# A two-layer transformer kernel: top-4 routing for four token blocks at once, and softmax sums read by the logarithm from PSUM

## The reference

```python
# layer 0: attention with 16 query and 4 key/value heads of 64, rotary embedding, no mask
attn = softmax(Q @ K.T / 8);  s = (attn @ V) @ Wo
# layer 0: feed-forward with 16 experts of width 512, plus a shared one of width 1024
scores = sigmoid(x @ router_weight.T)              # T x 16
# 2 of 4 groups by the sum of their two best scores; the others are set to 0
_, tidx = top_k(masked, 4)
tw = scores[tidx];  tw = 2.5 * tw / (sum(tw) + 1e-20)
routed = sum over experts of combine[t, e] * (silu(x @ gate_e) * (x @ up_e)) @ down_e
# layer 1: attention with 16 heads of 64 and a causal mask, with biases
# layer 1: feed-forward of width 3072 with integer weights * (1/127)
```

## Time and profile before

| what | value |
|---|---|
| timed runs | 5173.84 and 5219.94 us, median 5196.89 |
| profiled execution, slowest core | 4995.61 us |
| its span on the core read here (6), first to last instruction | 4994.0 us |
| spans of all cores | 4978.8 to 4994.0 us |
| TensorE matmul busy | 3663.9 us (73%), 14712 instructions |
| VectorE busy | 1323.1 us (26%), 2280 |
| ScalarE busy | 1394.9 us (28%), 1637 |
| chain that ended last | TensorE 53%, DMA 15%, VectorE 15%, ScalarE 10%, issue 5% |

### The profile page before, as it was taken

How to read it: one execution, slowest core, us unless ns; L and a number is a source line. 1 busy time by engine, 2 the same in 40 slices (tenths; PEclk the granted TensorE clock), 3 DMA queues, 4 the chain that set the end, 5 groups by cost and what they waited for, 6 DMA issues and landing times.

```text
span 4994.0 us, 44866 instructions; the slowest of 8 cores (4978.8 to 4994.0 us)
## 1 busy us (share of the span) xinstructions
PE 3663.9 (73%) x14712; PEld 1453.4 (29%) x14712; DVE 1323.1 (26%) x2280; ACT 1394.9 (28%) x1637; POOL 283.0 (6%) x522
## 2 busy tenths in 40 slices
PE   2126766799999999986777777742999966567775
PEld 0012222344434444432222222211444422122221
DVE  3442321033023113212122222225101023443332
ACT  1000000011011011103666666621111101555663
POOL 1000000000000000000000000001101000000000
PEclk7558888899999999998889888865999999889998
DMA  2127777844434434430011111134444420222122
GB/s 65 51 78 194 203 205 187 198 146 143 149 130 144 152 135 144 144 121 11 13 32 36 32 36 32 34 72 116 69 83 68 76 47 7 34 41 57 34 49 44
DMA packets 139090, 450.95 MB, mean 90 GB/s; under 512 B 15568, under 2 KB 15728, under 8 KB 122480
## 3 DMA queue, kind: packets, MB, share of 16 engines
q0 software_dynamic: 73632, 218.42, 21.3%
q1 hardware_dynamic: 65232, 229.67, 13.5%
HBM read 490.23 MB, written 73.40 MB: 113 GB/s over the span
## 4 chain that ended last, share of the span: by engine, by line
PE 53%; DMA 15%; DVE 15%; ACT 10%; issue 5%; DVEq 1%; SPq 0%; ACTq 0%; POOL 0%; POOLq 0%
ACT a16t L1481 9%; PE pst L738 8%; PE pst L752 8%; PE pst L854 4%; PE pb L854 4%; DMA a32t<-l_u 4%; PE pb L995 3%; PE pb L1430 3%; PE pst L931 3%; PE pst L942 3%; PE pst L1453 3%; PE pst L1458 2%; PE pb L1435 2%; PE pst L1347 2%; DMA a16t<-s_g 2%
## 5 line engine op out<-in xcount | busy, mean ns | idle before, releaser
L1481 ACT ACTIVATE a16t<-pst 128x1024 bf16<-128x1024 f32 x832 | 852.1, 1024 | 545.9 <-PE pst L1458 477.3
L738 PE MATMUL pst<-xn_sb,a16t 128*128 128x512 bf16 x2304 | 598.5, 407 | 177.1 <-DVE a16t L686 153.2
L752 PE MATMUL pst<-xn_sb,a16t 128*128 128x512 bf16 x2304 | 565.7, 390 | 0.0
L1430 PE MATMUL pb<-a16t 128*65 128x512 bf16 x832 | 343.9, 413 | 288.0 <-DVE a16t L1576 118.7
L765 ACT ACTIVATE a32t<-pst 128x512 f32<-128x512 f32 x288 | 172.0, 597 | 1103.6 <-PE pst L738 1103.6
L773 DVE TENSOR_TENSOR a32t<-a32t,pst 128x512 f32<-128x512 f32 x256 | 176.1, 688 | 1138.1 <-PE pst L752 1138.1
L1453 PE MATMUL pst<-a16t 128*128 128x512 bf16 x832 | 354.7, 426 | 162.6 <-DVE a16t L1392 103.8
L738 PEld LDWEIGHTS pst<-xn_sb,a16t 128*128 128x128 bf16 x2304 | 226.7, 102 | 496.2 <-issue 277.6
L1458 PE MATMUL pst<-a16t 128*128 128x512 bf16 x832 | 352.5, 424 | 0.0
L1435 PE MATMUL pb<-a16t 128*65 128x512 bf16 x832 | 344.6, 414 | 0.0
L752 PEld LDWEIGHTS pst<-xn_sb,a16t 128*128 128x128 bf16 x2304 | 232.5, 101 | 296.9 <-issue 44.6
(11 more groups left out here) (157 smaller groups left out, 2896.6 us busy)
## 6 DMA issues: line engine op xcount, KB each, us to landing
a16t<-s_g POOLq DMA_DIRECT2D x108, 512.0 KB, 5.0
a16t<-s_u SPq DMA_DIRECT2D x108, 512.0 KB, 4.2
a32t<-l_u SPq DMA_DIRECT2D x32, 1024.0 KB, 9.9
a16t<-s_d SPq DMA_DIRECT2D x27, 1024.0 KB, 5.6
a16t<-s_d POOLq DMA_DIRECT2D x27, 1024.0 KB, 6.1
s_g<-a16t SPq DMA_DIRECT2D x36, 512.0 KB, 7.4
s_u<-a16t SPq DMA_DIRECT2D x36, 512.0 KB, 8.4
s_d<-a16t SPq DMA_DIRECT2D x18, 1024.0 KB, 7.4
```

The source lines that it names most:

```text
L738: li = t.matmul(pb[gp_][:, :], a16t[:, o_gb[wp] + hc * 256 + ici * 128: o_gb[wp] + hc * 256 + ici * 128 + 128], xn_sb[:, hc * T + tc * TC: ...
L752: li = t.matmul(pb[up_][:, :], a16t[:, o_ub[wp] + hc * 256 + ici * 128: o_ub[wp] + hc * 256 + ici * 128 + 128], xn_sb[:, hc * T + tc * TC: ...
L1430: t.matmul(pb4[0:65, :], a16t[:, o_vtm + kc * 65 * nvh + kva * 65: o_vtm + kc * 65 * nvh + kva * 65 + 65], a16t[:, o_pt[kp]:o_pt[kp] + TC] ...
L1481: return s.activation(a16t[:, o_pt[kp]:o_pt[kp] + 2 * TC], pst[kp][:, 0:1024], AF.Exp, scale=0.125)
```

## The change

In stage A0, `f_top4` runs once per chunk on all 64 columns. The working arrays are viewed as 4 groups of 16. Maximum and sum reduce each group to one column (four results); the compares, which took the maximum as a per-partition scalar, are now two-tensor instructions whose second operand repeats the group's value 16 times; the final scale does the same with the reciprocal. The four transposes and the four copies stay, but stand behind the one top-4 operation instead of between four.

In stage C, of both layers, the two copies of the softmax sums and the one logarithm over 1024 columns go; two logarithms of 512 columns read the sums from PSUM instead. Operation `sums` is gone; those that named it now name `rcp`.

```diff
--- before.py
+++ after.py
@@ -531,42 +531,49 @@
                         return li
                     op_rt2 = P.add("V", f_rt2, deps=[op_rt1], name=f"A0rt2{tc}")
 
+                    def f_top4(v):
+                        cur = a32t[:, o_rs + 0:o_rs + 64]
+                        cur3 = cur.rearrange("p (g e) -> p g e", e=16)
+                        selb = a32t[:, o_rs + 64:o_rs + 128]
+                        selb3 = selb.rearrange("p (g e) -> p g e", e=16)
+                        ci = a32t[:, o_rs + 128:o_rs + 132]
+                        ci3 = ci.rearrange("p (g e) -> p g e", e=1)
+                        cib = ci3.broadcast_to((128, 4, 16))
+                        ci2 = a32t[:, o_rs + 132:o_rs + 136]
+                        ci2b = ci2.rearrange("p (g e) -> p g e", e=1)\
+                            .broadcast_to((128, 4, 16))
+                        mk = a32t[:, o_z:o_z + 64]
+                        mk3 = mk.rearrange("p (g e) -> p g e", e=16)
+                        sc3 = a32t[:, o_sc:o_sc + 64]
+                        Ct3 = a32t[:, o_Ct:o_Ct + 64].rearrange(
+                            "p (g e) -> p g e", e=16)
+                        v.tensor_copy(cur, mk)
+                        for _ in range(3):
+                            v.drain()
+                            v.reduce_max(ci3, cur3, axis=AX.X)
+                            v.drain()
+                            v.tensor_tensor(selb3, cur3, cib, ALU.is_ge)
+                            v.drain()
+                            v.scalar_tensor_tensor(cur, selb, -1e9, cur,
+                                                   ALU.mult, ALU.add)
+                        v.drain()
+                        v.reduce_max(ci3, cur3, axis=AX.X)
+                        v.drain()
+                        v.tensor_tensor(selb3, mk3, cib, ALU.is_ge)
+                        v.drain()
+                        v.tensor_tensor(cur, selb, sc3, ALU.mult)
+                        v.drain()
+                        v.reduce_sum(ci3, cur3, axis=AX.X)
+                        v.drain()
+                        v.tensor_scalar(ci, ci, 1e-20, None, ALU.add)
+                        v.drain()
+                        v.reciprocal(ci2, ci)
+                        v.drain()
+                        return v.scalar_tensor_tensor(Ct3, cur3, 2.5, ci2b,
+                                                      ALU.mult, ALU.mult)
+                    op_t4 = P.add("V", f_top4, deps=[op_rt2], name=f"A0t4{tc}")
+
                     for tt in range(4):
-                        def f_top4(v, tt=tt):
-                            cur = a32t[:, o_rs + rCUR:o_rs + rCUR + 16]
-                            ci = a32t[:, o_rs + rCI:o_rs + rCI + 1]
-                            ci2 = a32t[:, o_rs + rCI + 1:o_rs + rCI + 2]
-                            selb = a32t[:, o_rs + rSB:o_rs + rSB + 16]
-                            mk = a32t[:, o_z + tt * 16: o_z + (tt + 1) * 16]
-                            v.tensor_copy(cur, mk)
-                            for _ in range(3):
-                                v.drain()
-                                v.reduce_max(ci, cur, axis=AX.X)
-                                v.drain()
-                                v.tensor_scalar(selb, cur, ci[:, 0:1], None, ALU.is_ge)
-                                v.drain()
-                                v.scalar_tensor_tensor(cur, selb, -1e9, cur,
-                                                       ALU.mult, ALU.add)
-                            v.drain()
-                            v.reduce_max(ci, cur, axis=AX.X)
-                            v.drain()
-                            v.tensor_scalar(selb, mk, ci[:, 0:1], None, ALU.is_ge)
-                            v.drain()
-                            v.tensor_tensor(cur, selb,
-                                            a32t[:, o_sc + tt * 16: o_sc + (tt + 1) * 16],
-                                            ALU.mult)
-                            v.drain()
-                            v.reduce_sum(ci, cur, axis=AX.X)
-                            v.drain()
-                            v.tensor_scalar(ci, ci, 1e-20, None, ALU.add)
-                            v.drain()
-                            v.reciprocal(ci2, ci[:, 0:1])
-                            v.drain()
-                            return v.tensor_scalar(
-                                a32t[:, o_Ct + tt * 16: o_Ct + (tt + 1) * 16],
-                                cur, ci2[:, 0:1], 2.5, ALU.mult, ALU.mult)
-                        op_t4 = P.add("V", f_top4, deps=[op_rt2],
-                                      name=f"A0t4{tc}.{tt}")
 
                         def f_ctr(t, tt=tt):
                             dstb = pst1[:, 0:128] if tt % 2 == 0 else pst1[:, 512:640]
@@ -1527,26 +1534,19 @@
                         op_oevb = P.add("V", f_oevb, deps=[op_avl],
                                         name=f"C{L}oeb{qc}.{p}")
 
-                        def f_sums(s):
-                            s.copy(a32t[0:1, o_sums:o_sums + TC],
-                                   pb4[64:65, :])
+                        def f_rcp(s):
+                            s.activation(a32t[0:1, o_rcf:o_rcf + TC],
+                                         pb4[64:65, :], AF.Ln)
                             s.drain()
-                            return s.copy(
-                                a32t[0:1, o_sums + TC:o_sums + 2 * TC],
-                                pb5[64:65, :])
-                        op_sums = P.add("S", f_sums, deps=[op_avl, pv.get(("rcpd",))],
-                                        name=f"C{L}sums{qc}.{p}")
-
-                        def f_rcp(s):
-                            s.activation(a32t[0:1, o_rcf:o_rcf + 2 * TC],
-                                         a32t[0:1, o_sums:o_sums + 2 * TC], AF.Ln)
+                            s.activation(a32t[0:1, o_rcf + TC:o_rcf + 2 * TC],
+                                         pb5[64:65, :], AF.Ln)
                             s.drain()
                             return s.activation(a16t[0:1, o_nrm:o_nrm + 2 * TC],
                                                 a32t[0:1, o_rcf:o_rcf + 2 * TC],
                                                 AF.Exp, scale=-1.0)
-                        op_rcp = P.add("S", f_rcp, deps=[op_sums, pv.get(("bcd",))],
+                        op_rcp = P.add("S", f_rcp, deps=[op_avl, pv.get(("bcd",))],
                                        name=f"C{L}rcp{qc}.{p}")
-                        pv[("rcpd",)] = op_rcp
+                        op_sums = op_rcp
 
                         def mk_epi(op_rcp=op_rcp, blk=blk, qc=qc, p=p,
                                    pbread=(op_oeva, op_oevb, op_sums)):
```

## The result

| what | before | after |
|---|---|---|
| median of the timed runs | 5157.19 us (10 runs) | 4940.44 us (11 runs) |
| lowest and highest | 5000.24 and 5331.59 us | 4929.67 and 5291.10 us |
| ratio of comparable runs, 95% interval | | 0.9852 [0.9836, 0.9869] |

Some executions of either kernel run 3 to 7% longer, with a lower granted clock on the cores of one or both dies (among them the two timed runs known before the change, 5173.84 and 5219.94 us, and the profiled execution of the kernel after, 5267.14 us at 0.80 to 0.83 over the span), and the ratio compares only the others, 5000.2 to 5014.4 us before and 4929.7 to 4940.4 us after. The ratio is 74 us of about 5007 us (66 to 82).

A forecast was written before the change was run, and what follows sets the result against it. No single engine bounds the whole span: TensorE bounds the feed-forward stages, A0 is a chain. Gains of 59.5 + 2.2 = 61.7 us, taken from the timed median 5196.9, gave 5135 us; range for 8 in 10: 4925 to 5190.

The forecast's parts named there:

- the sum: Whole kernel: 59.5 + 2.2 = 61.7 us less, 4933.9 from the profiled execution's 4995.6, ratio 0.988.
- the gap of 3.6 to 4.5%: Whole kernel: two timed runs lay this far above the profiled execution; one in three that the changed kernel meets its level.
- Edit 1: Stage A0, top-4 for 64 columns at once: 14.87 us less per chunk, 59.5 us in four chunks.
- Both bounds of the range: Stage A0, top-4: gain 62.7 us if wide instructions cost what narrow ones do, 28 if each costs four.
- Edit 2: Stage C, softmax sums: ScalarE's chain 1.10 us shorter 64 times, showing only at each layer's last pair, 2.2 us.
- The slack of 0.67 us: Stage C, layer 1: the old chain ends at 4220.13, the next exponential waits for its scores and starts at 4220.80.
- hidden 62 times: Stage C: the 1.10 us shorter softmax-sums chain shows at only two of 64 head pairs, the last of each layer.
- A: Stage A0: wide forms are dear, a four-group reduction being done group by group; gain 28 to 50 us; chance 0.08.
- B: Stage A0: TensorE's clock stays up through the shorter pause, router matmuls finish sooner; gain 67 us, 5130; chance 0.08.
- C: Stage C: ScalarE's chain holds the first exponential at each pair; gain 130 us, 5067, faster by 2.5%; chance 0.04.
- D: Start of B0: a load coming when it came before eats the shift in A0; no gain, 5195 us; chance 0.05.
- E: B0 and B1, 1680 us: mean clock falls, each hundredth costing 17 us; at 0.88 5335, slower by 2.7%; chance 0.05.

The follow-up runs named there:

- sums_twice: The kernel before with each of the two copies of the softmax sums made twice, 1.28 us more in ScalarE's chain; measured ratio 1.0001 [0.9988, 1.0014].
- after_again: The kernel after, unchanged, run and profiled once more; measured ratio to the kernel before 0.9855 [0.9836, 0.9874].

## Why the prediction was right or wrong

**The level.** The forecast of 5135 us was wrong, and the step that failed is the last of the sum: the 61.7 us were taken from 5196.9, the median of the two timed runs known, and not from the 4995.6 of the profiled execution on which every row rested: 201 us too high. The sum's own figure, 4933.9, is 6.5 us from the measured median of 4940.4 and inside the 4929.7 to 4940.4 that the ratio compares. Part of that closeness is luck: 4995.6 lies about 11 us below the 5007 of the kernel before that the ratio compares, and the gain was forecast 12 us too small. The ratio of the sum, 0.988, doesn't have this luck, and its 0.9877 lies just outside 0.9836 to 0.9869. The prediction saw the gap of 3.6 to 4.5%, gave one in three for it, and let the range reach down to 4925; that alone made the range hold the time. An execution that is faster with the same instructions shows what the kernel can do; there was no row that could make it an outlier.

**Edit 1.** Right in mechanism and size. Block 4.86 us (forecast 4.91), L314 at 6.59 (6.57), A0 59.1 us shorter (59.5), first cast at 286.5 (near 290), still on the heels of the last copy. The slope from 16 to 32 columns held to 64: 0.23 us for a two-tensor instruction of 64 columns, forecast 227 ns, and 0.22 for a reduction over four groups. Both bounds of the range, 28 and 62.7, were wider than needed. The two-tensor form at 64 columns costs 0.22 to 0.23 us, no more than the scalar form at 16 (235 ns), so the swap cost nothing that shows. Whether the rule of the Trainium skill that was weighed there ("VectorE: DVE Perf Modes", section "The perf-mode tier table", half the rate for two-tensor forms in fp32) would make a scalar form of 64 columns cheaper, no run here shows.

**Edit 2.** Its local terms are right: 590 ns per logarithm (597 taken), ScalarE busy 1329.0 us (near 1330), two table loads, waits of L1555 for ScalarE 2.3 us less (2.2). The cover is there, as sums_twice shows. Two things were wrong. The slack of 0.67 us at the first exponential counts only in the first chunk of layer 1, at 7 changes of 31; at the other 24 the one at the broadcast, at least 1.55 us, does. That cost the forecast nothing, as edit 2 makes the chain shorter. And "hidden 62 times" priced the hidden pairs at nothing, while the low-clock stretches moved in them: 6.6 us came in the C0(+A1) stretch instead of 1.1, about 4 of them in its first 31 pairs. With the tail and edit 1 that makes 59.1 + 6.6 + 0.9, about 67, by the stages; the ratio says 74 with 6 to either side. The rest no row places; it is within what two profiles of one kernel differ by (C1: 720.8 to 733.3).

**The rivals.** A fell on the 0.22 us of the reduction. B's price, 67 us, lies near the measured gain, but its mechanism isn't there. The windows of the statistics in the kernel after, core 7, of the routing in the kernel before, core 0, of the statistics in after_again, core 1, and the router matmul of the kernel after:

```profile
87.00:103.00 16.00, 9.28 (x16) 3.73 (x16) 0.56 (x2) 4.41 (x7) 3.69 (x7) 1.00 0.42 105
```

```profile
66.00:101.00 35.00, 4.77 (x15) 1.90 (x13) 18.20 (x98) 4.03 (x8) 0.87 (x2) 1.00 0.03 6
```

```profile
87.00:103.00 16.00, 8.33 (x14) 3.48 (x14) 1.70 (x3) 3.77 (x6) 3.92 (x8) 0.50 0.49 116
```

```profile
L413 PE MATMUL pst<-xn_sb,cst x32: 585/631/631, 67.6 to 269.5; 128*128 128x512 bf16 x32
```

The 1.00 that was named as B's sign is printed on some cores, but the kernel before has it too, on five of its eight; the earlier trace rows came from one of the other three. It isn't a clock that stayed up: on those cores the trace holds no clock record yet (core 7 of the kernel after has its first at 270.0 us, core 0 of the kernel before at 347.7), and the view prints 1.00 where there is none. On every core with a record in that window, three of the kernel after and six of after_again, the statistics stand at 0.50, and the median router matmul takes 631 ns on the core shown. So B fell. C fell: 0.67 us of slack had become 1.79, and C1 didn't shorten. D fell: the first cast moved by the full amount. E fell: B0 and B1 keep their lengths (its 1680 us were the two windows of the earlier trace rows; the two stages are 2380 us long).

## What to carry to other kernels

Small VectorE instructions on a serial path cost by their number: 16 or 64 columns differ by 0.05 us, so groups that are worked one after the other should be put side by side and reduced with a view. Before calling a chain covered, follow its result to the first instruction that truly waits for it, in every kind of pair and not in one (here a mask made another instruction decide in one chunk of four), and measure the slack there; lengthening the chain until the time moves (1.28 us: nothing that the runs can tell, 3.85 us: 83 us) finds it better than shortening it. A change of 1 us at a pause can be worth more than itself, or less, by where TensorE's low-clock stretches fall afterwards: read the low-level time beside the lengths. When timed runs and the profiled execution of one kernel differ by more than the change can, make the forecast at the level whose rows it uses, and predict the ratio first.

## What the runs showed of the hardware

- A granted clock of 1.00 early in a profile can mean that there is no record. In stage A0 the same stretch reads 0.50 on some cores and 1.00 on others, in both kernels, with 631 to 634 ns for the median router matmul on all of them; the cores that read 1.00 have their first clock record later. From a core's first record on, record and pace agree in the kernel before: of the 112,474 bf16 matmuls of 512 columns that lie within one record, each takes over 0.55 us at 0.50 and under 0.45 us at 1.00, without an exception on the eight cores.
- Low-clock stretches shift against the work when another engine's timing changes, by 1.1 us less or by 3.85 us more. At one pair of C0 the clock over 8 us was 0.50 to 0.66 on 31 of 32 cores before, 0.89 to 0.92 on all 32 with the shorter chain and 0.89 to 0.91 on all 8 with the longer one, and the pair 1.2 of 31 us shorter on the mean; over the 31 pairs of C0 13.0 us less at the low level went with 4.0 us less time. In C1 two copies moved from VectorE to ScalarE took the low-level time from 141 to 46 us and 53 us off the stage.
- Repeating a value 16 times as a second operand costs nothing that shows (0.22 to 0.23 us for such a compare, 0.23 us for the dense product beside it), and a reduction of 4 x 16 columns takes no longer than these.
